# A two-layer attention and feed-forward kernel: one low part in every third step moves from GpSimd to VectorE, with waits by piece for the last weight and another written order

## What is computed

```python
x = x + L0_xattn(layernorm(x), ctx)     # energy = (ctx Wq + bq)(ctx Wk + bk)^T, softmax, x_m = x attention^T
x = x + L0_ffn(layernorm(x))            # rms norm, 8-bit rows, ternary weights, value * silu(gate), 8-bit rows, out
x = x + L1_xattn(layernorm(x), ctx)     # 16 heads of 128 over 8 key/value heads, mask, softmax, Wo
x = x + L1_ffn(layernorm(x))            # weights rounded to fp8 (e4m3), silu(gate) * up, down, three scales
```

## Time and profile before

| | |
|---|---|
| three executions | 319.19, 320.16, 320.66 us (median 320.16) |
| the profiled execution | 319.45 us, its span 317.4 us |
| TensorE matmuls | 294.9 us busy, 93% of the span, 1981 records |
| VectorE | 252.2 us, 79% |
| ScalarE | 258.5 us, 81% |
| GpSimd | 217.9 us, 69% |
| mean granted TensorE clock | 0.993 of full speed |
| largest DMA use | 108 writes to and 54 reads from the turning room in DRAM |

### The profile page before, as it was taken

One profiled execution on the slowest core, in us unless ns is written; L12 is line 12 of the kernel. 1 busy time (PEld: TensorE's weight loads), 2 busy tenths in 40 slices (PEclk: granted clock), 3 DMA queues, 4 the chain that ended last, 5 costly groups with the idle time before them and its releaser, 6 DMA issues.

```text
span 317.4 us, 6401 instructions
## 1 busy us (share of the span) xinstructions
PE 294.9 (93%) x1981; PEld 258.8 (82%) x1992; DVE 252.2 (79%) x713; ACT 258.5 (81%) x607; POOL 217.9 (69%) x290
## 2 busy tenths in 40 slices
PE   3676999999999999999989999999999999999994
PEld 2465566889988987899779989889999998989784
DVE  3789698989888789888889788897877595766674
ACT  0869796489999989999997897788899998975350
POOL 3786663566887788797877897878897696772001
PEclk9999799999999999999999999999999999999999
DMA  7994602002046867678637566687665466200201
GB/s 219 380 350 135 176 0 68 1 1 76 5 81 179 245 168 199 165 209 202 180 88 207 150 179 162 165 221 203 147 188 151 116 197 200 69 2 0 68 1 66
DMA packets 54609, 44.59 MB, mean 140 GB/s; under 512 B 11696, under 2 KB 45104, under 8 KB 54576
## 3 DMA queue, kind: packets, MB, share of 16 engines
q1 hardware_dynamic: 54016, 43.93, 49.1%
q10 hardware_dynamic: 560, 0.26, 0.3%
HBM read 27.01 MB, written 15.20 MB: 133 GB/s over the span
## 4 chain that ended last, share of the span: by engine, by line
PE 21%; ACT 15%; POOL 8%; issue 5%; DVE 1%; ACTq 0%; POOLq 0%; DVEq 0%
PE pb L2015 14%; PE pb L2278 4%; ACT sm L980 4%; POOL tp_lo L666 4%; ACT pT_hi L992 3%; PE pb L2312 2%; POOL xn L588 1%; ACT sm L998 1%; ACT L980 1%; POOL sm L661 1%; ACT L1019 1%; ACT fuse L1019 1%; ACT q_hi L975 1%; ACT oT_hi L1004 1%; POOL rstd L582 1%
## 5 line engine op out<-in xcount | busy, mean ns | idle before, releaser
L666 POOL TENSOR_TENSOR tp_lo<-tp,pT_hi 128x512 fp32r<-128x512 f32 x54 | 69.2, 1297 | 20.9 <-ACT pT_hi L992 20.8
L980 ACT ACTIVATE sm<-sm,smin 128x256 f32<-128x256 f32 x128 | 63.6, 503 | 1.1 <-DVE smin L1563 0.7
L1563 DVE CUSTOM_DVE_ANT_0 sm<-pb,mask_all 128x256 f32<-128x256 f32 x128 | 47.5, 419 | 4.0 <-PE pb L2015 3.6
L1580 DVE STREAM_TRANSPOSE blocks<-sm 128x1024 f32<-128x1024 f32 x27 | 33.5, 1240 | 7.0 <-DMA block_room<-blocks 6.1
L2015 PE MATMUL pb<-ctx_hi,q_hi 128*128 128x256 f32 x128 | 37.8, 295 | 0.5 <-DVE q_lo L1550 0.4
L2015 PE MATMUL pb<-xT_hi,m_hi 128*128 128x256 f32 x128 | 37.2, 291 | 0.1
L2015 PE MATMUL pb<-n_hi,oT_hi 128*128 128x256 f32 x128 | 37.1, 290 | 0.1
L2015 PE MATMUL pb<-xT_hi,m_lo 128*128 128x256 f32 x128 | 36.2, 283 | 0.0
L2015 PE MATMUL pb<-xT_lo,m_hi 128*128 128x256 f32 x128 | 36.2, 283 | 0.0
L2015 PE MATMUL pb<-ctx_hi,q_lo 128*128 128x256 f32 x128 | 36.2, 282 | 0.0
L2015 PE MATMUL pb<-ctx_lo,q_hi 128*128 128x256 f32 x128 | 36.1, 282 | 0.0
(11 more groups left out here) (195 smaller groups left out, 946.4 us busy)
## 6 DMA issues: line engine op xcount, KB each, us to landing
block_room<-blocks SPq DMA_DIRECT2D x108, 128.0 KB, 2.5
tp<-block_room SPq DMA_DIRECT2D x54, 256.0 KB, 3.1
w_raw<-in_w SPq DMA_DIRECT2D x4, 576.0 KB, 4.2
wraw<-in_wgvT SPq DMA_DIRECT2D x4, 512.0 KB, 7.4
wraw<-in_woutT SPq DMA_DIRECT2D x2, 512.0 KB, 10.6
out<-xb SPq DMA_DIRECT2D x4, 256.0 KB, 2.2
xa<-in_x SPq DMA_DIRECT2D x3, 256.0 KB, 4.6
xb<-in_ctxT SPq DMA_DIRECT2D x2, 256.0 KB, 6.1
```

The source lines that it names most:

```text
L666: g.tensor_tensor(tp_lo[:, z, c, :], tp[:, z, c, :], as_f32(pT_hi[:, c, :]), ALU.subtract).then_inc(pT_lo_pool, 1)
L980: a.activation(sm[:, n % 2, k, :], sm[:, n % 2, k, :], ACT.Exp, bias=smin[:, n % 2, k:k + 1], scale=-1.0, accum_out=ssum[:, n % 2, k:k + 1 ...
L1563: v.tensor_tensor_reduce(out=sm[:, n % 2, k, :], in0=bank(passing_bank("s", 2 * n + h))[:, (k % 2) * S:(k % 2 + 1) * S], in1=mask_all[:, b ...
L1580: v.transpose(blocks[:].rearrange("p g k b -> p k g b"), sm[:, n % 2, :, :].rearrange("p k (g b) -> p k g b", b=32)).then_inc(blocks_done, 1)
```

## The change

- `low_by_pool` gives half 0 of the steps 3, 6, ... 27 (nine steps) to VectorE; GpSimd keeps the other 45 halves.
- Every `down` of the first half of the tokens waits for the pieces of the weight that it reads (12 to 16 of them), in place of one wait for all 16 in `down(0, 0)`.
- All five lists and the bank list are written in another order. Work is neither added nor left out: GpSimd's list is nine entries shorter, VectorE's nine longer, the others are as long as before.

```diff
         def low_by_pool(n, c):
-            return by_blocks(n) and (True)
+            return by_blocks(n) and (c == 1 or n % 3 != 0)
...
             def down(c, n):
                 h, i = divmod(c, KI)
                 pe.wait_ge(f_lo_done, c + 1)
+                if c < KI:
+                    pe.wait_ge(w8_done, -(-(2 * KD * INNER + (i + 1) * D) // PIECE))
                 if c == 0 and n == 0:
-                    pe.wait_ge(w8_done, B * EIGHTS)
                     left, count = left_bank(last_passing(3))
                     pe.wait_ge(left, count)
```

The start of the SP list:

```diff
             projection(1)
+            projection(0)
             contexts(0)
-            projection(0)
             rows(1)
             rows(2)
+            gate_value(1)
             rows(3)
             gate_value(0)
             gate_value(2)
-            gate_value(1)
             gate_value(3)
+            scales()
+            hidden_out(0)
             contexts(1)
-            hidden_out(0)
+            raw(5)
+            raw(1)
+            raw(2)
+            mask_bytes()
+            norm_weight()
             raw(0)
-            norm_weight()
-            mask_bytes()
-            raw(4)
-            raw(5)
-            raw(6)
-            raw(1)
             hidden_out(1)
             raw(3)
+            raw(4)
+            raw(6)
```

Further down this list `scales()` is gone from behind `eighth(3)`, `eighth(2)` goes from ahead of `blocks_written(10)` to behind `blocks_read(12)`, `eighth(3)` from behind `blocks_read(19)` to behind `blocks_read(13)`, and some writes and reads of neighbouring steps change places. The start of ScalarE's list:

```diff
+            context_high(0)
             projected1(0)
-            context_high(0)
             values_high(0)
+            sums(0)
+            exps1(0)
             rows1(0)
-            exps1(0)
             projected1(1)
-            sums(0)
             sums(1)
             probs1(0)
             rows1(1)
             exps1(1)
             projected1(2)
+            rows1(2)
+            projected1(3)
+            probs1(1)
+            exps1(2)
+            sums(2)
             ternary(0)
-            probs1(1)
-            projected1(3)
+            turned_kv(0)
             ternary(1)
-            exps1(2)
             ternary(2)
-            sums(2)
-            rows1(2)
-            turned_kv(0)
-            turned_kv(1)
-            turned_kv(2)
             transposed(0)
             ternary(3)
```

On TensorE `value_half(0, 0)` and four more halves now stand ahead of `mix(2)`, and `turn_kv(1)` to `turn_kv(3)` behind the gates of rows 0; later, for step 11, `attn_out(10, 0)` stands between `contexts(11, 0)` and `contexts(11, 1)`, where the two contexts were neighbours, and `down(0, 1)`, `down(1, 1)` and `down(2, 1)` are spread among the steps 28 to 30. ScalarE's list around that step:

```diff
             silu(7)
+            probs(11, 0)
             outputs(10)
-            probs(11, 0)
             exps(14, 0)
+            probs(11, 1)
             rows3(2)
-            probs(11, 1)
```

More of the change, by code:

```diff
@@ L520, in _ @@
             blocks_read(12)
+            eighth(2)
             blocks_written(13)
@@ L535, in _ @@
             blocks_read(18)
+            blocks_read(19)
             blocks_written(20)
-            blocks_read(19)
-            eighth(3)
-            scales()
+            blocks_written(21)
             blocks_read(20)
-            blocks_written(21)
             blocks_read(21)
             blocks_written(22)
+            blocks_read(22)
             blocks_written(23)
-            blocks_read(22)
+            blocks_read(23)
             blocks_written(24)
-            blocks_read(23)
             blocks_written(25)
@@ L730, in _ @@
             normalise(3)
[L731 removed]
             outputs_split(5)
[L733 to L739 removed]
+            normalise(4)
+            eighths_out(1)
+            normalise(5)
+            rows3(1)
+            probs_low(3, 1)
+            outputs_split(6)
             eighths(2)
@@ L1881, in _ @@
+            second(6)
             inverse(20)
-            masked(21, 0)
+            q_low(22)
             outputs_low(16)
-            masked(21, 1)
-            q_low(22)
-            second(6)
+            added3(1)
             second(7)
             inverse(21)
+            third_stats(3)
             turn_blocks(20)
-            added3(1)
-            third_stats(3)
             outputs_low(17)
+            probs_low(18, 0)
+            q_low(23)
             masked(22, 0)
+            third_low(3)
@@ L1894, in _ @@
             masked(22, 1)
-            q_low(23)
+            turn_blocks(21)
             stats4(1)
-            third_low(3)
+            masked(23, 0)
+            q_low(24)
+            masked(23, 1)
+            outputs_low(18)
             inverse(22)
-            turn_blocks(21)
-            masked(23, 0)
-            masked(23, 1)
-            q_low(24)
+            eighths(10)
+            turn_blocks(22)
             rows4_low(0)
-            outputs_low(18)
-            eighths(10)
+            q_low(25)
@@ L1977, in _ @@
             probs_low(31, 1)
+            eighths(15)
+            outputs_low(31)
             fuse_low(3)
-            outputs_low(31)
+            fuse_low(4)
             added3(3)
@@ L2561, in _ @@
             attn_out(16, 1)
+            rows3(3)
             attn_out(17, 0)
-            rows3(3)
+            contexts(18, 0)
             attn_out(17, 1)
-            contexts(18, 0)
+            contexts(18, 1)
             scores(23, 0)
-            contexts(18, 1)
+            queries(24)
             scores(23, 1)
-            queries(24)
             queries(25)
             contexts(19, 0)
-            contexts(19, 1)
             scores(24, 0)
             scores(24, 1)
+            contexts(19, 1)
+            rows4(1)
+            queries(26)
             attn_out(18, 0)
-            queries(26)
-            rows4(1)
             attn_out(18, 1)
@@ L2635, in _ @@
             contexts(27, 1)
+            attn_out(26, 0)
+            up4(4)
+            attn_out(26, 1)
             scores(31, 0)
+            contexts(28, 0)
+            contexts(28, 1)
             scores(31, 1)
-            attn_out(26, 0)
-            attn_out(26, 1)
-            contexts(28, 0)
-            up4(4)
-            contexts(28, 1)
-            down(0, 1)
-            down(1, 1)
-            down(2, 1)
             attn_out(27, 0)
             attn_out(27, 1)
+            attn_out(28, 0)
+            down(0, 1)
             contexts(29, 0)
+            down(1, 1)
             contexts(29, 1)
@@ L2651, in _ @@
             probs4(30, 1)
-            attn_out(28, 0)
+            down(2, 1)
             attn_out(28, 1)
@@ L2673, in _ @@
             down(4, 0)
+            down(3, 1)
             rows4(3)
```

878 lines of the change are left out of this document (438 added, 440 removed), and 46 rows, old and new, of the table PASSING.

## The result

Four executions of the changed kernel beside four of the kernel before gave 323.36 us (322.57 to 326.07) against 319.96: a ratio of 1.012, with a 95% interval from 1.0083 to 1.0158. So the change costs 3.4 to 4.7 us; the forecast was 318.3, and its range ended at 322.6. The profiled execution took 323.42 us, its span 321.6.

What follows compares the result with a forecast made beforehand. TensorE was taken as the bound, busy 294.9 of 317.4 us, gains only from its 22.5 us idle. Share 0.4, middle 0.9 and start 0.6 sum to 1.9 us: 318.3 us against 320.16, range 314.8 to 322.6.

Steps and rivals of the forecast that it cites:

- The share: Nine `tp_lo` subtractions moved from GpSimd to VectorE, about 1.0 us each: 0.4 us gained, bounds 0.8 gained to 1.2 lost.
- the cover: On VectorE, the nine subtractions' 9 us in all were taken as covered by its 65 us of idle time.
- The port rival: VectorE's nine subtractions and GpSimd hold each other at the shared port, delaying TensorE: 321.9 us, chance 0.07.
- The middle: New order in the middle: 0.7 us gained at step 11, 0.2 at step 7, sum 0.9; bounds 5.0 gained, 1.5 lost.
- Of the other idle time of the middle (3.4 us) I change nothing: TensorE's remaining middle idle time was left at 3.4 us, since every removed stall can have a new one beside it.
- two steps ahead of its use: A block write behind a waiting `blocks_read` delays VectorE's next turning, which is two steps ahead of its use; priced at nothing.
- The start: First gates on TensorE begin 0.4 to 0.8 us early: 0.6 us gained, with up to 3 us gained as bound.
- the landing of `wout`: In the start, the last piece of `wout` lands at 24.0 us instead of 25.1, as less data is loaded ahead.
- the point of 32.0: In the start, the time in us of the first gate at which the new order breaks even: 35.2 - 3.2.
- The late-`wout` rival: In the start, `wout` lands at 26.5, first gate at 33.7 to 34.1, more half clock: 322.4 us, chance 0.13.
- The rest at nothing: The waits of `down` by piece, the small transfers on SP's queue and ScalarE's table loads: no gain or loss.
- The signs: What the changed profile would show if right (first gate before 32 us, middle idle near 4) or wrong (new waits).

Runs made afterwards that it cites:

- share_only: The kernel before with only VectorE's nine subtractions added, no other order changed: 2.4 us slower at the medians, 2.0 by the ratio.
- changed_again: The changed kernel itself, measured again beside other kernels: ratio 1.0141 to the kernel before (1.0107 to 1.0174).
- sums_behind: The changed kernel with `sums(2)` back behind `ternary(2)` on ScalarE: 3.2 us slower than the changed kernel.
- both_behind: The changed kernel with `sums(2)` behind `ternary(2)` on ScalarE and `weight_sums(1)` behind `scaled(0)` and `ternary(3)` on VectorE: 0.8 us faster than the change, inside the intervals.
- steps_3_10_new: The kernel before with the change's lists for steps 3 to 10 alone, GpSimd making all low parts: that stretch took 79.65 us, 7.2 more than in the change.

## Why the prediction was wrong, point by point

- **The share (forecast 0.4 us gained).** The duration was right: 0.83 us on the mean against the 1.0 taken. The lock with GpSimd as seen in the earlier trace rows showed in the change at its worst as 1.12 us, in share_only three times as 1.43 to 1.80 us. The step that failed is the cover. I set nine operations against 65 us of idle time. Idle time of an engine in the sum covers nothing at the place. Alone the share costs 2.0 to 2.4 us; in the new order taking it back costs 2.3 us or more. The port rival needed over 1.5 us per operation on the mean and had 0.83 in the change and 1.06 in share_only, so it is not what decided; in share_only the lock is part of the cost.
- **The middle (0.9 us gained).** At step 11 the wait fell to 0.63 us where I had 0.4, and its remedy alone gave 0.5 us for my 0.7, with an interval that holds nothing. The wait at step 7 is gone. The failing step is "Of the other idle time of the middle (3.4 us) I change nothing", and with it "two steps ahead of its use" for the turning. I had priced the waits removed and none that the order made. I looked at TensorE's waits alone; VectorE's own waits showed in the kernel before that ten of 27 transposes already stood for the writes: a resource in use to the end, which any reordering would strain. Steps 3 to 31 lost 2.5 us in the profile of the change, beyond my bound of 1.5, and 1.1 us in that of changed_again, within it; either way there was a loss where I had a gain of 0.9. The 0.4 to 0.6 us of it in steps 21 to 31 have no cause shown.
- **The start (0.6 us gained).** The mechanism, the gates waiting for `wout` through `sums(2)`, was the one priced; the term that failed is the landing of `wout`. I put it at 25.1 before and 24.0 after. The last update of that transfer's semaphore came at 26.08 us before and at 26.34 after. The first microsecond of this error is a misread row: 10.6 us in the earlier trace rows is the middle of two transfers, and the second took 11.6.

```profile
DMA to landing us min/median/max: 9.5/10.6/11.6
```

The rest is the 1.1 us that less data ahead was to bring and didn't. The transfers of this queue landed one behind the other, a piece of 512 KB every 1.3 to 1.5 us; one such piece fewer stood ahead, but the last weight piece ahead of the scales landed 0.5 us later than before (14.13 against 13.66), and the two small scales landed at about 14.3 and 15.6. I had priced all scales by their bytes at 0.4 us; these are the page's rows for the two:

```profile
gsc<-in_gate_scale SPq DMA_DIRECT2D x1, 3.0 KB, 8.1
usc<-in_up_scale SPq DMA_DIRECT2D x1, 3.0 KB, 8.8
```

That they held up the pieces behind them is likely, but no run moved them alone. The steps from the landing to the first gate took 6.5 us in place of my 7.2 to 7.6. So the gate came at 32.82, 0.8 us past the point of 32.0, where I had 0.4 to 0.8 ahead. The late-`wout` rival had its place and nearly its 26.5 us, and had a chance of only 0.13. That its result (322.4) was near is in part luck: it had the gate at 33.7 to 34.1, a longer stretch at half clock, which the profile of the change has not, and a gain of 1.4 us from the middle, which lost instead. What I also missed is VectorE's `weight_sums(1)` ahead of `scaled(0)`. And the price of half clock in the start was too high: 3.4 us of it were taken as 1.7 us, but the profile of before, which has them, reached `scores(3, 1)` at 83.43 us, 0.3 to 0.7 us behind the four kernels with the old start and the full clock.
- **The rest at nothing** was right. From `rows4(3)` to the last matmul it took 19.15 us against 19.06, and `rows4(3)` waited 0.4 us where it had waited 0.59.
- **The signs** I named were the right ones: new waits for `q_lo` and `oT_lo` over 1 us together, and `sums(2)` waiting beyond 25 (until 26.36), both came. Of the signs of being right the nine rows on VectorE came (0.66 to 1.12 us), while the first gate came behind 32 us and the middle idled 7.2 us, not 4.

## What to carry to other kernels

Before a written order is changed, list the rounds that close through a single buffer (here transpose, four writes, landing, next transpose) and compare their length with the step: where they are near to each other, look for the waits that a new order makes around them, and try a second buffer first: here it was worth 3.5 us in the new order and 1.1 us in the old, more than any of the reorderings tried. Cover is a matter of place: name the instruction behind the inserted one and who waits for it. And a share of work between engines belongs to the order it was written with: here the share alone and the order without the share both lost.

## What the runs showed of the hardware

The granted clock of the start differs from execution to execution of one kernel. In changed_again TensorE had been busy for 0.77 us of the 2 us from 20 and for 1.41 us of the next 2, in which the clock fell to half, 1.2 of 2.4 GHz (windows, columns as above):

```profile
20.00:22.00 2.00, 0.77 (x4) 0.34 (x2) 1.90 (x10) 2.00 (x8) 1.06 (x2) 1.00 0.80 300
22.00:24.00 2.00, 1.41 (x6) 0.99 (x7) 1.71 (x4) 0.65 (x2) 2.00 (x3) 0.94 0.82 302
24.00:26.00 2.00, 1.31 (x5) 0.86 (x4) 1.17 (x3) 1.20 (x4) 1.80 (x5) 0.50 1.03 384
28.00:30.00 2.00, 2.00 (x7) 1.30 (x6) 0.73 (x3) 2.00 (x3) 0.00 (x0) 0.50 0.43 163
```

In the first profile of the same kernel TensorE stood 2.92 us ahead of 29.48, and the clock stayed at full. Of 85 executions of the kernel before, 14 had a mean clock of 0.99 or less; of the ten of the changed kernel, 4; of sums_behind, where TensorE stood 5.7 us at one place, all 5. Within the changed kernel these four took 325.1 us on the mean and the other six 323.4. So idle time in the start seems to be paid twice, the second time by chance. An estimate from these numbers makes it some 0.5 us of the loss (0.4 x 1.7 us, less 0.16 x 1.1 us before, where 320.6 stand against 319.5). That the new start is the cause isn't shown: the count for the changed kernel is of ten executions, both_behind, also with most of the new start, had none in 5, and steps_3_10_new, with the old start, had 4 in 6, its profiled stretch at half clock behind the 3.0 us wait in step 9.
